# Bilinear pair interaction and a three-layer tower: one in eight of the wide products' sums moved from ScalarE to VectorE, with new places for transposes, tower steps and groups

## What is computed

```python
p = inputs[:, rowidx]
q = inputs[:, colidx]
out = jnp.einsum('bie,fie,bif->bi', p, param, q)
...
h = jnp.concatenate([z, dense_ctx], axis=1)
h = jnp.maximum(h @ W_top1 + b_top1, 0.0)
h = jnp.maximum(h @ W_top2 + b_top2, 0.0)
y = h @ W_top3
```

## Time and profile before

| | us |
|---|---|
| median of 3 runs (1274.24 to 1276.26) | 1275.0 |
| the profiled execution | 1274.6 |
| its span | 1272.8 |

### The profile page before, as it was taken

How to read it: one execution, slowest core, us unless ns; L and a number is a source line. 1 busy time by engine, 2 the same in 40 slices (tenths; PEclk the granted TensorE clock), 3 DMA queues, 4 the chain that set the end, 5 groups by cost and what they waited for, 6 DMA issues and landing times.

```text
span 1272.8 us, 23705 instructions
## 1 busy us (share of the span) xinstructions
PE 1231.0 (97%) x6064; PEld 481.1 (38%) x6064; DVE 1023.4 (80%) x1680; ACT 1023.9 (80%) x7945; POOL 577.7 (45%) x615
## 2 busy tenths in 40 slices
PE   6788999999999999999999999999999999999999
PEld 3233433333333343333344333433343333343333
DVE  5768999998887777888787887788889787788980
ACT  0049988777488989998958999899968898999981
POOL 5555555555555555555345555555225554000000
PEclk9989999999999999999999999999999999999999
DMA  6311422132221222222221222122112122111100
GB/s 173 94 46 46 143 72 70 45 94 64 71 70 48 70 71 70 49 67 64 66 67 47 73 69 71 45 70 72 54 59 69 46 70 67 30 47 50 44 2 0
DMA packets 33201, 80.88 MB, mean 64 GB/s; under 512 B 11773, under 2 KB 12285, under 8 KB 32937
## 3 DMA queue, kind: packets, MB, share of 16 engines
q1 hardware_dynamic: 12320, 57.17, 13.9%
q0 software_dynamic: 19456, 19.96, 7.7%
q10 hardware_dynamic: 1288, 2.24, 0.6%
HBM read 79.32 MB, written 0.01 MB: 62 GB/s over the span
## 4 chain that ended last, share of the span: by engine, by line
PE 60%; ACT 31%; issue 3%; DMA 2%; POOL 2%; DVE 1%; another core or an unknown queue 1%; ACTq 0%
ACT wide_prod L541 29%; PE ring L727 26%; PE z_ps L750 13%; PE ring L732 11%; PE ring L756 7%; DMA rows<-tbl,idx_now 2%; POOL rows L481 2%; PE ring L701 2%; ACT e_t L502 1%; PE ring L760 1%; DMA idx_now<-idx 0%; DVE prod L606 0%; PE ring L763 0%; PE ring L708 0%
## 5 line engine op out<-in xcount | busy, mean ns | idle before, releaser
L541 ACT ACTIVATE wide_prod<-wide_prod 128x64 f32<-128x64 f32 x3904 | 933.7, 243 | 52.4 <-DVE wide_prod L619 25.6
L481 POOL DMA_INDIRECT rows<-tbl,idx_now x608 | 576.9, 949 | 496.7 <-DMA rows<-tbl,idx_now 292.2
L541 ACT ACTIVATION_READ_ACCUMULATOR wide_prod<-wide_prod 128x1 f32 x3904 | 739.4, 189 | 24.4 <-issue 23.4
L606 DVE TENSOR_TENSOR prod<-ring,e_t 128x512 f32<-128x512 f32 x1008 | 630.8, 683 | 147.6 <-PE ring L727 101.1
L727 PE MATMUL ring<-e_t,w 64*128 64x512 f32 x2176 | 563.0, 609 | 9.6 <-ACT e_t L502 5.9
L619 DVE TENSOR_TENSOR wide_prod<-ring,rows 128x512 f32<-128x512 f32 x512 | 328.3, 682 | 44.6 <-PE ring L732 33.3
L727 PEld LDWEIGHTS ring<-e_t,w 64*128 64x128 f32 x2176 | 215.9, 187 | 300.1 <-issue 203.7
L732 PE MATMUL ring<-w,e_t 64*128 64x512 f32 x1024 | 292.1, 607 | 11.4 <-ACT e_t L502 7.1
L750 PE MATMUL z_ps<-prod,strip 128*32 128x512 f32 x2096 | 256.2, 603 | 0.1
L732 PEld LDWEIGHTS ring<-w,e_t 64*128 64x128 f32 x1024 | 106.2, 186 | 147.0 <-issue 86.7
L750 PEld LDWEIGHTS z_ps<-prod,strip 128*32 128x32 f32 x2096 | 55.3, 109 | 182.0 <-issue 119.6
(11 more groups left out here) (23 smaller groups left out, 79.3 us busy)
## 6 DMA issues: line engine op xcount, KB each, us to landing
w<-weights SPq DMA_DIRECT2D x64, 768.0 KB
rows<-tbl,idx_now POOLq DMA_INDIRECT x608
w<-weights SPq DMA_DIRECT2D x4, 512.0 KB
z_t<-tbl SPq DMA_DIRECT2D x8, 224.0 KB
w<-w1z SPq DMA_DIRECT2D x1, 1792.0 KB
h<-hot_ids ACTq DMA_DIRECT2D x6, 256.0 KB
z_t<-hot_ids ACTq DMA_DIRECT2D x2, 256.0 KB
w<-w2p SPq DMA_DIRECT2D x1, 512.0 KB
```

Source lines behind the costliest of these rows:

```text
L481: nc.gpsimd.indirect_dma_start(out=rows[:, slot, t, E * f:E * f + E], out_offset=None, in_=tables[m * 2 + f], in_offset=bass.IndirectOffse ...
L541: last = nc.scalar.activation(products, products, ACT.Copy, accum_out=z_b[:, h, t, col:col + 1])
L606: nc.vector.tensor_tensor(dst[:, j, :], ring[:, bank, :], e_t[:, k, :], ALU.mult).then_inc(t_free, 1)
```

## The change

Three tables of places and one rule change; no function does.

```diff
--- before.py
+++ after.py
@@ -77,11 +77,11 @@
 
 
 
-TILE_AT = [-23, -14, -14, -1, -1, 8, 8, 8, 20, 20, 29, 37, 56, 66, 75, 75, 112, 112, 150, 171]
-STEP_AT = [33, 50, 90, 103, 126, 137, 165]
+TILE_AT = [-26, -26, -14, -4, 8, 8, 8, 8, 20, 20, 29, 38, 53, 68, 75, 75, 112, 112, 148, 174]
+STEP_AT = [33, 52, 88, 101, 126, 138, 162]
 TURN_LAG = 14
 
-GROUP_LAG = [8, 7, 6, 5, 7, 5, 3, 6, 5, 5, 5, 6, 6, 6, 5, 5, 4, 4, 4, 5, 4, 5, 4, 5, 4, 5, 5, 5, 4, 4, 4, 3, 5]
+GROUP_LAG = [8, 8, 7, 5, 8, 6, 3, 6, 6, 6, 5, 4, 3, 4, 3, 5, 3, 4, 3, 5, 4, 7, 5, 3, 4, 5, 3, 4, 4, 5, 3, 3, 5]
 BEHIND_LAST = 8
 
 
@@ -244,7 +244,7 @@
 def reduced_by_vector(c, v):
 
     m, t = WIDES[v]
-    return c == 0 and (t == 3 and m < 12 or t == 1 and m < 8)
+    return c == 0 and (t == 3 and m < 12 or t == 1 and m < 8) or c > 0 and v % 8 == 7
 
 
 def fixed_slot(c):
```

## The result

The changed kernel takes 1265.5 us (median of 9 runs) where the kernel before takes 1274.2 in the same comparison (9 runs): ratio 0.9928, 95% interval 0.9905 to 0.9951. It is faster, inside the range, by 9 us and not by the 17.6 forecast. The profiled execution takes 1267.7 us, its span 1265.9, against 1274.6 and 1272.8.

The account below looks back on a forecast made before the run. PE was taken as the bound, losing some 37 us in chunks 1 to 3, about 21 on ACT and 16 on DVE. Terms -17.9 - 2.1 + 2.4 = -17.6 from 1274.6 gave 1257 us, range 1250 to 1267.

Parts of the forecast that it names:

- all four clusters: Late ACT copies at tile 12, tile 18, tiles 1 and 2, tiles 14 and 15; all predicted to go, -17.9 us.
- nine places: Places in chunks 1 to 3 where PE waits on late copies of turned tiles, 17.9 us lost together.
- -17.9: Term for moved copies: PE's waits on ACT's late tile copies in chunks 1 to 3 all go, 17.9 us saved.
- I take 0.1 ... +2.4: Cost of moving 24 sums to DVE: 0.1 us exposed per reduce, 2.4 us in all.
- the other 16 us: Part of PE's 37 us lost in chunks 1 to 3: items that wait for DVE's products, 16 us.
- 72 idle waits stand against 24 reduces: Reason for the small reduce price: DVE sat idle 89 us in 72 waits, to cover 24 reduces of 1.21 us.
- the forecast's 74: Weight loads of line 727 whose releaser was DVE, cited for the 16 us of items waiting on DVE's products.
- Chunk 0 keeps its items and sums; I allow 1 us either way: Chunk 0 was priced at nothing, with 1 us allowed either way.
- -2.1 for the detours: PE leaves the items 186 times instead of 195: 1.4 us from seven tiles behind groups, 0.7 from two joined tiles.
- The second: Rival: copies late elsewhere, at tile 13 or tiles 19, 0 and 1; half of 17.9 returns, 1266 us, chance 0.23.
- The third: Rival: DVE's waits shrink too, half of the 16 us goes, 1249 us, chance 0.14.
- The fifth: Rival: slower, DVE sets the pace, 1284 us; decides from 0.83 us exposed a reduce; chance 0.06.

Follow-up runs that it names:

- set A: The first comparison, the only one traced for the forecast's check: changed kernel 1265.5 us against the kernel before at 1274.2, ratio 0.9928.
- set C: Another chip, kernel before 1261.4 us. Ratios: change again 0.9977, reduces doubled 1.0063, old lags everywhere 1.0040, old lags in chunk 0 plus tiles 9, 10 later 0.9911.
- set D: Another chip, kernel before 1239.6 us. With tiles 9, 10 later: kernel before 1.0009, change 0.9983, change without 24 sums 1.0014; reduces before detours 0.9993.
- set B: Another chip, kernel before 1247.5 us. Ratios: change with old lags in chunk 0 0.9977, rule alone 1.0101, places alone 1.0173, change without 24 sums 0.9992.

## Why the prediction was right and wrong

**Right:** the way, the range, and, in set A, the main mechanism. ACT's waits at all four clusters went; of nine places only tiles 14 and 15 of chunk 3 still lose 1.0 us. L541 x3520, L630 x36 at 1209 ns, detours as counted. ACT's loss fell by 15.7 us, by the forecast's own way of counting by up to 20; the term was -17.9. Part of the 17.9 was matmuls at half the clock in the wake of a late copy, at two of the places (granted 0.50 from 622.7 to 626.1 and from 1059.6 to 1063.0 in the trace before); the forecast's reading of the starts took it all for the copies' lateness, and both went together. That 1265.5 lies inside the range owes something to set A, too: in set C the same change is 0.2% faster than the kernel before, which is as little as the forecast thinks can be told from no change.

**Mis-sized: "I take 0.1 ... +2.4" and the other 16 us as if they stayed.** In set A DVE's share of the loss rose by 4.6 us (8 by the forecast's sharing). The ground given, "72 idle waits stand against 24 reduces", says that DVE has idle time, not that it is behind the reduce: the same reduce costs 1.22 at place 191 with the old tables, 0.0 with the new ones where nothing pauses, and 0.6 when it is the second of two. Nor do weight loads with DVE as releaser size such a loss: in chunks 2 and 3 the kernel before has 52 of the forecast's 74 and loses 8.9 us by DVE; in set D, with tiles 9 and 10 later, it has 62 there and loses 2.2. That the rise in A comes from reduce and pauses together, each using the slack of the other, is what the table suggests; it wasn't isolated there.

**Mis-sized: "Chunk 0 keeps its items and sums; I allow 1 us either way".** It lost 4.7. The lags hold for chunk 0 too, where other items stand; some 1.7 of it is theirs, as sets B, C and D agree. The rest is about what tile 12's late copy (2.8 us) and the two items at half the clock behind it (1.5) took, in that traced execution and in no other trace.

**Borne out as far as it can be seen: -2.1 for the detours.** By the forecast's own prices and the two orders, 0.8 of it stands in each of the chunks 0 to 2, and chunk 3 has 0.2 more, since tile 4 is now turned in it and no longer in the chunk before. So chunks 2 and 3 should gain 0.5; in set D the two kernels differ there by 0.2, with 0.5 more lost, which makes 0.7.

**What no term held.** The -17.9 were taken as a property of the order. In set D, where ACT doesn't pause, the kernel before (tiles 9 and 10 later) hardly loses at these places, and in sets B and D the kernels nearest to the change (old lags in chunk 0, or tiles 9 and 10 later) are 0.2% faster than the kernel before. The trace of before had the sign of it: tile 18 loses 1.6 and 1.8 us in chunks 1 and 2 and nothing in chunk 3, where the gathers are over. The sum as measured in set A: -15.7 by ACT, +4.6 by DVE, -0.6 of saved detours and what rounding leaves, +4.7 in chunk 0: the span's -7.

**The rivals.** The second named the time, 1266, but not its cause: tile 13's copy came 0.07 to 1.1 us ahead of its first use and cost PE at most 0.1, and the three banks at 174 cost nothing. The third is wrong by its sign, DVE's waits grew. The fifth needed 0.83 us a reduce; even the second of a pair cost 0.62. On the page whose rule spoke for it, the Trainium skill's "VectorE: DVE Perf Modes", section Rules for kernel authors (tensor_reduce is the slowest operation): at 1207 to 1212 ns for 1024 elements it was no slower by element than products (two of 512 start 600 ns apart), in any run; where it stands in the queue decided, not what it is.

## What to carry to other kernels

Idle time of an engine covers new work only where the two meet in its queue: find for each inserted instruction the wait that it falls into, and where there is none (five units in a row), price it in full. Before a stall is put down to the order, look at whether the same instructions pause by themselves; a gain taken from such a stall is one of that occasion. A stretch where the disturber is silent, here the end of the last chunk behind the last gather, prices the order alone. And a table that holds for several stages must be priced in each.

## What the runs showed of the hardware

The same kernel took 1274, 1261, 1247 and 1240 us in four sets, 2.8% apart. In the traces (of kernels near to each other) the granted clock and the back-to-back times are alike (0.99; an item 0.86 us, DVE's products 600 ns apart in A as in D); what differs are the pauses of ACT and DVE, up to 47 us in ACT's sums, nearly all of ACT's 0.9 to 1.8 us after the last issue of a half gather and none behind the last gather. Gathers at 13 us a tile become the bound where PE is faster and they themselves are later: 11 to 12 us of wait in set B at a place with some 4 us to spare in set A, and after it matmuls at half the clock.
